# Attention's first loads, norm and projections moved into the last recurrent steps of a four-block kernel

## The chip, the cores and the metric

One core of a Trainium2 chip runs the whole program. The time is device microseconds (us) of that core, the median of several runs. Beside it stands one execution that the hardware profiler recorded.

## The reference

Three recurrent blocks (RWKV-like, width 512, 32 heads of 16) are followed by one cross attention over a context of 1024 rows; batch 4, 512 tokens, all float32. Cut to what matters here:

```python
x = block0(x); x = block1(x); x = block2(x)      # norm, token shift, lora mixes, r k v g w, scan, group norm, Wo, norm, FFN
a = layer_norm(audio_kv, ln_gamma, ln_beta)       # (4, 1024, 512): depends on the context alone, not on x
Q = (x @ Wq.T), K = (a @ Wk.T), V = (a @ Wv.T)    # 16 heads of 32
scores = einsum('bhtd,bhsd->bhts', Q, K) * scale, masked with -inf
out = softmax(scores) @ V @ Wo.T
return x + tanh(gate) * out
```

The norm of the context, K and V can be computed before the recurrent blocks are done; Q of batch 0 needs the first batch's x alone.

## The kernel before, in words

Everything is laid out by hand: each engine's instructions stand in program order, and semaphores tie them together. No scheduler decides anything.

**Recurrent part.** 24 units (3 layers, 2 time halves, 4 batches; `ITS` is 24) go through a software pipeline: in step `s` (from -1 to 25) unit `s+1` is normed, mixed and projected (`norm_a`, `lora`, `stream`), unit `s` is scanned (`products`, `updates`, `outputs`, `normed_back`), unit `s-1` has its output product and second norm (`out_product`, `norm_c`), and unit `s-2` its FFN (`feed`). In step 23 the first of these is empty, in step 24 the first two, and in step 25 only the FFN of the last unit is left. The weights (1 MB each) come through three slots on GpSimd's queue; activations are loaded and stored on SyncE's queue (SP), the finished units to a DRAM tensor `xs`.

**Attention.** Its buffers (`AT_AT`, `k_side`, `q_side`) lie over those of the recurrent part. `FIRST` lists batch 0's preparing tiles: two means, the variance, two spreads of 1/std (`rstd0`, `rstd1`), the first K tiles `k00`, `k01`, the first Q tile `q0`, and eight V tiles `v0` to `v7`; a tile is one PSUM bank that TensorE fills. K and Q come in four column groups per batch (`k{e}0`, `k{e}1`, `q{e}`); each group serves four heads, and 4 token blocks times 4 heads make 16 **turns** of a group, 64 of a batch, 256 in all (`HEADS`). A turn is `scores` (2 matmuls), maximum on VectorE, exponential on ScalarE, and three turns later eight transposes (`turned`); each fourth turn has `weighted`. Before a group's first turn its K and Q, split by ScalarE and VectorE into two rounded parts (`first_part`, `second_part`), are copied head by head into `k_side` and `q_side` by 16 + 16 small DMAs (`side_by_side`), all on SP's queue. Everything else for the later groups and the next batch is slipped in between turns: the table `BESIDE` says after which turn which tile is filled, and which engine work follows. Keys are (block, head); (10, 2) is turn 42 of the batch.

SP's queue in the attention of batch b is: side copies of groups 1, (store of the batch before), 2, 3, then the next batch's context (2 MB, `load_context`), x for its queries, mask, x for the residual, and the side copies of the next batch's group 0.

**Start.** GpSimd builds `ident` and `blk` and zeroes three large buffers; its last memset counts to `const_ready`, for which TensorE, VectorE, ScalarE and SP wait before anything else.

Of the kernel before, what the change touches and what calls it, by code (L numbers as in the profile page):

```python
# [13 lines left out]
P = 128  # L14
# [54 lines left out]
BESIDE = {(0, 2): [(0, "k10")], (1, 0): [(0, "k11")], (1, 2): [(-1, "wo0")], (2, 0): [(-1, "wo1")], (2, 2): [(0, "q1")], (3, 0): [(-1, "wo2")],  # L69
# [4 lines left out]
FIRST = ["mean0", "mean1", "var", "rstd0", "rstd1", "k00", "k01", "q0"] + [f"v{n}" for n in range(ST)]  # L74
PARTS = [f"{w}{e}{n}" for e in range(KT) for w, n in (("k", 0), ("k", 1), ("q", ""))]


def beside(n):
    if not 0 <= n < HEADS:
        return []  # L80
    b, u, h = n // (TT * KT * HPT), n // HPT % (TT * KT), n % HPT
    return [(b + off, name) for off, name in BESIDE.get((u, h), ()) if 0 <= b + off < B]

# [52 lines left out]
CONSTS = 11  # L136


def laid_out():
# [15 lines left out]
    for i, name in enumerate(("th", "thg", "tdh", "st_a")):  # L155
# [11 lines left out]
         "wv": (14320, SLOT), "wq": (16368, SLOT), "vals": (18416, ST * 384), "vals3": (21488, 2 * ST * P), "k_part": (23536, 2 * SK), "q_part": (25584, 2 * T),  # L167
         "astd": (26608, SQ), "mx": (26864, 8), "den": (26880, 2 * HPT), "rden": (26888, HPT), "rb": (26896, 2 * P), "rt": (27152, P), "ay": (27504, KT * T), "ao0": (29552, KT * T),
         "ao1": (31600, KT * T), "xq": (33648, KT * T), "probs": (48048, 4096)}
# [81 lines left out]
def build(nc, a):  # L251
    ctx = ExitStack()
    with ctx:
# [87 lines left out]
        const_ready = sem("const_ready")  # L341
        start_loaded = sem("start_loaded")
# [64 lines left out]
        at_loaded = sem("at_loaded")  # L407
# [6 lines left out]
        side_loaded = [sem(f"side_loaded{n}") for n in range(2)]  # L414
# [14 lines left out]
        def side_at(group):  # L429
            return 16 * 2 * HPT * HPT * (group // 2 + 1)  # L430
# [17 lines left out]
        def _(sp):  # L448
# [3 lines left out]
            sp.dma_start(part_of("s_first"), a["s_first"]).then_inc(start_loaded, 16)  # L452
            sp.dma_start(small_w, a["small"][0]).then_inc(small_loaded, 16)
# [21 lines left out]
            def load_vm(it, pair):  # L475
                if pair == 0:
                    sp.wait_ge(*b_ring.empty_at(it, "VT1"))
                    if it:
# [6 lines left out]
            sp.wait_ge(const_ready, CONSTS)  # L485
            load_x1(0)
            load_xl(1)
            for s in range(ITS + 2):
                e, c, b, n = s - 2, s - 1, s, s + 1
                if b < ITS:  # L490
                    load_vm(b, 0)
                if 1 <= n < ITS - 1:
                    load_xl(n + 1)
                if b < ITS:
                    load_vm(b, 1)
                if e >= 0:
                    store_x(e)
                if 0 < b < ITS:
                    load_x1(b)
                if n < ITS and n % UNITS_PER_LAYER == UNITS_PER_LAYER - 1 and n + 1 < ITS:  # L500
                    for name in ("w2g1", "td2_1"):
                        sp.wait_ge(a_ring.full, a_ring.full_at(n, name))
                    sp.dma_start(small_w, a["small"][layer_of(n + 1)]).then_inc(small_loaded, 16)
# [29 lines left out]
            def side_by_side(group):  # L533

                b, e = group // KT, group % KT
                sp.wait_ge(*d_ring.empty_at(b, f"k{e}1"))
# [3 lines left out]
                for g in range(HPT):  # L540
                    for h in range(HPT):
                        to, of = slice(AD * g, AD * g + AD), slice(AD * h, AD * h + AD)
                        sp.dma_start(k_side[group % 2][to, h, :], k_part[of, K_PART[g], :]).then_inc(side_loaded[group % 2], 16)
                sp.wait_ge(*d_ring.empty_at(b, f"q{e}"))
                for g in range(HPT):
                    for h in range(HPT):
                        to, of = slice(AD * g, AD * g + AD), slice(AD * h, AD * h + AD)
                        sp.dma_start(q_side[group % 2][to, h, :], q_part[of, Q_PART[g], :]).then_inc(side_loaded[group % 2], 16)  # L548
# [5 lines left out]

            sp.wait_ge(x_stored, X_STORED)
            load_context(0)
            for n, name in enumerate(("wk", "wq", "wv", "wo")):
                sp.dma_start(view(name), a["at_w"][n]).then_inc(at_loaded, 16)
            sp.dma_start(lnp[:], a["at_ln"]).then_inc(at_loaded, 16)
            sp.dma_start(gate[:, 0:1], a["gate"]).then_inc(at_loaded, 16)  # L560
            load_xq(0)
            load_mask(0)
            side_by_side(0)
# [17 lines left out]
        def _(pe):  # L581
# [216 lines left out]
            for n in ("s1", "m1", "s2", "i1"):  # L798
                norm_a(0, n)
            for s in range(-1, ITS + 2):  # L800
                e, c, b, n = s - 2, s - 1, s, s + 1
                has_e, has_c, has_b, has_n = 0 <= e < ITS, 0 <= c < ITS, 0 <= b < ITS, n < ITS
                if has_e:
                    feed(e, "fr", 0)
                    feed(e, "fk", 0)
                if has_b:
                    products(b, "P0a")
                    products(b, "P0b")
                if 0 < n and has_n:
                    norm_a(n, "s1")  # L810
                if has_b:
                    values_by_token(b)
                if 0 < n and has_n:
                    norm_a(n, "m1")
                if has_b:
                    products(b, "P1")
                    products(b, "P2a")
                if has_e:
                    feed(e, "fr", 1)
                if has_b:  # L820
                    products(b, "P2b")
                if 0 < n and has_n:
                    norm_a(n, "s2")
                if has_c:
                    out_product(c, 0)
                if has_b:
                    products(b, "P4a")
                if 0 < n and has_n:
                    norm_a(n, "i1")
# [1048 lines left out]
```

## Time and profile before

| | us |
|---|---|
| median of 3 runs | 3555.29 (3549.32 to 3556.19) |
| profiled execution, its own time | 3555.04 |
| its span, first to last instruction | 3553.2 |
| TensorE busy | 3326.4 (94%) |
| VectorE busy | 2632.3 (74%) |
| ScalarE busy | 1861.2 (52%) |
| GpSimd busy | 109.9 (3%) |
| mean granted clock of TensorE | 0.968 |

The span is what the change is counted in: the run's own time is 1.84 us longer than it. Busy shares are means over stages with different limits, so the rows further down are read by stage. The recurrent part ends at 2504.95 with TensorE's last FFN matmul, the first score matmul starts at 2595.12, and attention goes on to the end.

### The profile page before, as it was taken

To read this page: it belongs to the slowest core of one execution; us is meant where nothing else is said; L and a number is where in the kernel's file an instruction comes from. 1 tells how busy PE (TensorE), PEld (TensorE's weight loads), DVE (VectorE), ACT (ScalarE), POOL (GpSimd) and SP (SyncE) were. 2 spreads that over 40 slices of the span, in tenths; PEclk is the share of its full clock that TensorE was granted. 3 is DMA by queue.
4 is the path that set the end of the run, shared out by engine and by line. 5 is a ranking of instruction groups with operands and counts; after the bars stand their busy time and mean duration, and the time that the engine had idled before them with its cause. 6 is when DMAs were issued, how large, how long until landed. Compare 5 with 4: busy or idle time off the path is not lost.

```text
span 3553.2 us, 74824 instructions
## 1 busy us (share of the span) xinstructions
PE 3326.4 (94%) x31856; PEld 2507.2 (71%) x31856; DVE 2632.3 (74%) x3721; ACT 1861.2 (52%) x3087; POOL 109.9 (3%) x204
## 2 busy tenths in 40 slices
PE   6899999999999999999999999996697997997998
PEld 4667777778787777777878777775355565665666
DVE  3788888888888888888888888875155565465566
ACT  2455554555555555555555555443155555555555
POOL 1000000000000000000000000000000000000000
PEclk9899999999999999999999999998799999999999
DMA  3113332232333333233233223222324133132221
GB/s 119 60 67 108 108 120 96 105 134 91 107 117 108 108 108 109 102 123 120 90 108 116 97 108 120 94 97 78 110 54 107 48 75 94 37 84 85 60 70 51
DMA packets 91914, 336.65 MB, mean 95 GB/s; under 512 B 16704, under 2 KB 37824, under 8 KB 65600
## 3 DMA queue, kind: packets, MB, share of 16 engines
q0 software_dynamic: 27648, 201.34, 15.7%
q1 hardware_dynamic: 63936, 130.52, 12.6%
q8 instruction: 255, 4.18, 0.5%
q14 instruction: 75, 0.61, 0.1%
HBM read 252.11 MB, written 16.78 MB: 76 GB/s over the span
## 4 chain that ended last, share of the span: by engine, by line
PE 86%; DVE 6%; ACT 3%; SPq 2%; DMA 2%; issue 1%; POOL 0%; ACTq 0%; DVEq 0%; POOLq 0%
PE psum L704 39%; PE psum L713 5%; PE psum L773 5%; PE psum L750 4%; PE psum L976 4%; PE psum L952 3%; PE psum L942 3%; PE psum L994 3%; PE psum L966 2%; SPq L548 2%; PE psum L957 2%; PE psum L948 2%; PE psum L659 2%; DVE psum L1734 1%; PE psum L669 1%; PE psum L609 1%
## 5 line engine op out<-in xcount | busy, mean ns | idle before, releaser
L704 PE MATMUL psum<-rw 128*128 128x256 f32 x6144 | 1421.7, 388 | 19.5 <-DVE rw L1435 10.6
L704 PEld LDWEIGHTS psum<-rw 128*128 128x128 f32 x6144 | 1172.8, 194 | 234.5 <-issue 52.8
L1547 DVE TENSOR_TENSOR rw<-rw 128x2048 f32<-128x2048 f32 x192 | 429.5, 2279 | 18.7 <-ACT rw L1151 16.7
L1734 DVE CUSTOM_DVE_ANT_0 psum<-psum,mem 128x1024 f32<-128x1024 f32 x256 | 313.5, 1225 | 114.1 <-PE psum L966 114.0
L1310 ACT ACTIVATE rest<-psum,mem 128x1024 f32<-128x1024 f32 x256 | 284.9, 1113 | 72.7 <-DVE mem L1734 70.8
L976 PE MATMUL psum<-ident,rest 128*128 128x128 f32 x2048 | 272.7, 276 | 3.9 <-DVE mem L1704 3.8
L976 PEld LDWEIGHTS psum<-ident,rest 128*128 128x128 f32 x2048 | 236.7, 142 | 44.2 <-issue 13.5
L1096 ACT ACTIVATE rw<-psum 128x512 f32<-128x512 f32 x192 | 111.5, 593 | 297.3 <-PE psum L704 297.1
L1429 DVE SCALAR_TENSOR_TENSOR rw<-psum,rw 128x256 f32<-128x256 f32 x480 | 196.4, 477 | 72.6 <-PE psum L659 52.8
L1034 ACT ACTIVATE rw<-rw 128x256 f32<-128x256 f32 x192 | 99.8, 590 | 273.5 <-DVE rw L1379 273.5
L966 PE MATMUL psum<-side 128*128 128x512 f32 x512 | 212.3, 496 | 30.5 <-ACT rest L1310 22.6
L1303 ACT ACTIVATE mem<-psum 128x512 f32<-128x512 f32 x256 | 151.8, 593 | 159.3 <-PE psum L976 159.3
L713 PE MATMUL psum<-rw 128*128 128x512 f32 x432 | 220.7, 612 | 14.4 <-DVE rw L1517 8.4
L1530 DVE TENSOR_TENSOR_SCAN rw<-rw 128x2112 f32<-128x2112 f32 x48 | 218.7, 4556 | 16.5 <-ACT rw L1134 16.5
L1134 ACT ACTIVATE rw<-psum 128x512 f32<-128x512 f32 x192 | 197.7, 1141 | 28.5 <-PE psum L750 28.4
L773 PE MATMUL psum<-rw 128*32 128x128 f32 x6144 | 200.2, 277 | 6.1 <-DVE rw L1547 6.1
L1739 DVE COPY mem<-psum 128x512 f32<-128x512 f32 x256 | 176.0, 687 | 35.6 <-PE psum L976 35.4
L1151 ACT ACTIVATE rw<-rw 128x1024 f32<-128x1024 f32 x96 | 191.6, 2070 | 0.0
L773 PEld LDWEIGHTS psum<-rw 128*32 128x32 f32 x6144 | 161.4, 111 | 37.8 <-issue 17.4
L750 PE MATMUL psum<-rw 32*32 32x128 f32 x6144 | 180.8, 274 | 1.2 <-ACT rw L1134 1.2
L1812 POOL DMA_DIRECT2D rw<-big_dram x192 | 101.5, 529 | 2355.0 <-PE psum L704 2342.5
L750 PEld LDWEIGHTS psum<-rw 32*32 32x32 f32 x6144 | 142.0, 105 | 41.4 <-issue 39.1
(149 smaller groups left out, 4389.7 us busy)
## 6 DMA issues: line engine op xcount, KB each, us to landing
rw<-big_dram POOLq DMA_DIRECT2D x192, 1024.0 KB, 5.1
side<-mem SPq DMA_DIRECT2D x256, 128.0 KB, 2.4
rw<-xs_dram SPq DMA_DIRECT2D x32, 512.0 KB, 3.3
side<-mem SPq DMA_DIRECT2D x256, 64.0 KB, 2.0
rw<-rw SPq DMA_DIRECT2D x192, 64.0 KB, 1.9
xs_dram<-rw SPq DMA_DIRECT2D x24, 512.0 KB, 2.7
rw<-x_dram SPq DMA_DIRECT2D x16, 512.0 KB, 3.3
mem<-ctx_dram SPq DMA_DIRECT2D x4, 2048.0 KB, 8.1
```

Of the source, the lines that this page charges most:

```text
L704: last = mm(t[:, o * TC:(o + 1) * TC], big[:, k, P * m:P * m + P], src[:, k, 0:TC], start=k == 0, stop=k == KT - 1, skip_group_check=True)
L713: b_ring.fill(mm(t, blk, src, start=True, stop=True), it, name)
L750: last = mm(t[32 * g:32 * g + 32, k, :, :, s], k_t[rows, s, 256 * pair + at:256 * pair + at + 32], v_m[rows, s, :, at:at + 32], start=True ...
L773: last = mm(t[32 * q:32 * q + 32, o, s, :], rz[:, k, c, 32 * m:32 * m + 32], s_bd[:, half, NM * i + m, :], start=False, stop=c == 3, skip_ ...
L966: last = mm(t[:, sh, :], q_side[group % 2][:, h, P * q:P * q + P].bitcast(F32R), k_side[group % 2][:, h, sh * 512:sh * 512 + 512].bitcast( ...
L976: last = nc.tensor.transpose(tokens(t, o), tokens(probs[:, n % HPT, :], first + o), ident[:])
L1134: b_ring.empty(f(to, t, ACT.Copy), it, f"U{pair}{q}")
L1310: s_ring.empty(f(probs[:, n % HPT, :].rearrange("p (a s) -> p a s", a=2), s_ring.bank(n, "s"), ACT.Exp, scale=-1.0, bias=mx[:, n % 8:n % 8 ...
L1429: last = stt(to[:, m, :], t[:, o * TC:(o + 1) * TC], par(layer, MAAS, KT * FAN[s] + m), sxa[:, m, :], ALU.add, ALU.mult)
L1530: state_dve.inc(nc.vector.tensor_tensor_scan(s_flat, d_flat, s_flat, 0.0, ALU.mult, ALU.add), it, f"scan{pair}")
L1547: state_dve.inc(tt(s_bd[:, half, :, :].rearrange("p c (h j) -> p c h j", h=4), own, place, ALU.mult), it, f"b{k}{half}")
L1734: maxima.inc(nc.vector.tensor_tensor_reduce(t, t, mbias.rearrange("p (a s) -> p a s", a=2), 1.0, 3.4e38, ALU.add, ALU.min, accum_out=mx[:, ...
```

## The change

1. **Start.** The three memsets of `v_m`, `rz`, `d_in` move behind the first three weight loads on GpSimd's queue and get a semaphore of their own (`zeroed`), which only their first users await. ScalarE now waits at its start for five small loads instead of three (the norm parameters `lnp` and `gate` are loaded there), and computes tanh(gate) there.
2. **First loads.** Context, `wk` and mask of batch 0 are issued on ScalarE's queue at the start of step 23; `wv`, `wq` and the query x on SP's queue before step 24's store; `wo` after the recurrent loop. Buffers are rearranged so that these lie over what is free by then.
3. **First tiles.** Batch 0's means are filled in step 23 before the second half of `fv`, the variance, `q0` and `rstd` at its end; `k00`, `k01` and `v0` to `v4` in step 24. `v5` to `v7` of each batch move into the next 64 turns, after turns 0, 1 and 2.
4. **Side copies.** The 256 K copies go to GpSimd's queue, behind all weight loads; the 256 Q copies stay on SP's. Their semaphores are split (`k_laid`, `q_laid`).
5. **The table and SP's order.** `BESIDE` is keyed by turn and spreads the tiles differently; the next batch's context load is issued ahead of the side copies of group 3.

```diff
-BESIDE = {(0, 2): [(0, "k10")], (1, 0): [(0, "k11")], (1, 2): [(-1, "wo0")], (2, 0): [(-1, "wo1")], (2, 2): [(0, "q1")], (3, 0): [(-1, "wo2")],
...
+BESIDE = {0: [(0, "v5")], 1: [(0, "v6")], 2: [(0, "v7")], 4: [(0, "k10")], 6: [(0, "k11")], 8: [(0, "q1")], 10: [(-1, "wo0")], 14: [(-1, "wo1")],
...
+FIRST = ["mean0", "mean1", "var", "q0", "rstd0", "rstd1", "k00", "k01"] + [f"v{n}" for n in range(5)]
...
# SP: new, called in step 24 ahead of store_x; then side_by_side(0)
+            def next_loads():
+                last = ITS - 1
+                sp.wait_ge(b_ring.full, b_ring.full_at(last, "P4d"))
...
+                sp.dma_start(view("wv"), a["at_w"][2]).then_inc(at_loaded["wv"], 16)
+                sp.wait_ge(b_ring.full, b_ring.full_at(last, "KT1"))
+                sp.dma_start(view("wq"), a["at_w"][1]).then_inc(at_loaded["wq"], 16)
+                sp.wait_ge(o_ring.full, o_ring.full_at(last, "O1"))
+                sp.wait_ge(x_stored, 16 * (ITS - UNITS_PER_LAYER + B + 1))
+                load_xq(0)
# SP: attention
             for b in range(B):
                 side_by_side(KT * b + 1)
+                side_by_side(KT * b + 2)
                 if b:
                     store(b - 1)
-                side_by_side(KT * b + 2)
+                if b + 1 < B:
+                    load_context(b + 1)
                 side_by_side(KT * b + 3)
                 if b + 1 < B:
-                    load_context(b + 1)
                     load_xq(b + 1)
                     load_mask(b + 1)
# TensorE
-            pe.wait_ge(at_loaded, 6 * 16)
-            for name in FIRST:
-                batch_tile(0, name)
+                if s == ITS - 1:
+                    batch_tile(0, "mean0")
+                    batch_tile(0, "mean1")
                 if has_e:
                     feed(e, "fv", 1)
...
+                if s == ITS - 1:
+                    batch_tile(0, "q0")
+                    batch_tile(0, "rstd0")
+                    batch_tile(0, "rstd1")
# ScalarE
+            def first_loads():
+                last = ITS - 1
+                act.wait_ge(a_dve.sem, a_dve.at(last, "mix_g"))
...
+                nc.scalar.dma_start(view("an"), a["ctx"][0]).then_inc(cx_loaded, 16)
+                nc.scalar.dma_start(view("wk"), a["at_w"][0]).then_inc(at_loaded["wk"], 16)
+                nc.scalar.dma_start(mask_u, a["mask"][0:1, :].broadcast_to((P, SK))).then_inc(mask_loaded, 16)
...
+                if s == ITS - 1:
+                    first_loads()
                 if has_e:
                     feed(e, "fr", 0)
# VectorE, step 23: ahead of scan(b, 1), and at the step's end
+                if s == ITS - 1:
+                    centred(0, 0)
+                    centred(0, 1)
...
+                if s == ITS - 1:
+                    inverse(0)
                 if has_c:
                     norm_c(c, "mix")
                 if has_b:
                     gated(b, 0)
                     gated(b, 1)
+                if s == ITS - 1:
+                    after(0, "q0")
+                    scaled(0, 0)
+                    scaled(0, 1)
# GpSimd
-            nc.gpsimd.memset(part_of("v_m"), 0.0)
-            nc.gpsimd.memset(part_of("rz"), 0.0)
-            nc.gpsimd.memset(part_of("d_in"), 0.0).then_inc(const_ready, 1)
             for turn, (it, which) in enumerate(weights):
+                if turn == NSLOT:
+                    nc.gpsimd.memset(part_of("v_m"), 0.0).then_inc(zeroed, 1)
+                    nc.gpsimd.memset(part_of("rz"), 0.0).then_inc(zeroed, 1)
+                    nc.gpsimd.memset(part_of("d_in"), 0.0).then_inc(zeroed, 1)
...
+            for group in range(GROUPS):
+                b, e = group // KT, group % KT
+                if group >= 2:
+                    pool.wait_ge(s_ring.full, s_ring.full_at(HPT * TT * (group - 1) - 1, "s"))
+                elif group == 1:
+                    pool.wait_ge(x_stored, X_STORED)
+                pool.wait_ge(*d_ring.empty_at(b, f"k{e}1"))
+                for g in range(HPT):
+                    for h in range(HPT):
+                        to, of = slice(AD * g, AD * g + AD), slice(AD * h, AD * h + AD)
+                        nc.gpsimd.dma_start(k_side[group % 2][to, h, :], k_part[of, K_PART[g], :]).then_inc(k_laid[group % 2], 16)
```

On TensorE, from step 24 to the first scores, before. `L704` is a projection of the recurrent part, `L598`, `L620`, `L604`, `L609` the second norm; `L931` the means, `L922` the variance, `L936` rstd, `L942` K, `L948` Q, `L952` V, `L966` scores:

```order
L704 MATMUL psum<-rw 128x256 x56
L598 MATMUL psum<-rw,ones 32x256 x4
L704 MATMUL psum<-rw 128x256 x8
L620 MATMUL psum<-rw 128x256
L604 MATMUL psum<-rw,ones 32x64 x16
L609 MATMUL psum<-rw,pick 128x64 x4
L704 MATMUL psum<-rw 128x256 x48
L931 MATMUL psum<-mem,ones 128x512 x8
L922 MATMUL psum<-mem,ones 32x256 x16
L936 MATMUL psum<-mem,pick 128x256 x4
L942 MATMUL psum<-mem 128x512 x8
L952 MATMUL psum<-mem 128x512 x32
```

The same stretch of TensorE now, where `L718` is the recurrent projection, `L612`, `L634`, `L618`, `L623` the second norm, `L848` K, `L858` V and `L878` scores:

```order
L718 MATMUL psum<-rw 128x256 x24
L848 MATMUL psum<-mem 128x512 x8
L718 MATMUL psum<-rw 128x256 x32
L612 MATMUL psum<-rw,ones 32x256 x4
L858 MATMUL psum<-mem 128x512 x4
L718 MATMUL psum<-rw 128x256 x8
L634 MATMUL psum<-rw 128x256
L858 MATMUL psum<-mem 128x512 x4
L618 MATMUL psum<-rw,ones 32x64 x16
L858 MATMUL psum<-mem 128x512 x4
L623 MATMUL psum<-rw,pick 128x64 x4
L858 MATMUL psum<-mem 128x512 x8
```

Two K tiles and five V tiles now stand between step 24's matmuls, and 48 of `L718` (step 25) follow directly, with the scores behind them.

On SP's queue, in the attention of batch 0, before (`L543` K copies, `L548` Q copies, `L509` context, `L518` x, `L514` mask):

```order
L543 DMA side<-mem 32x1024 x16
L548 DMA side<-mem 32x512 x16
L543 DMA side<-mem 32x1024 x16
L548 DMA side<-mem 32x512 x16
L543 DMA side<-mem 32x1024 x16
L548 DMA side<-mem 32x512 x16
L509 DMA mem<-ctx_dram 128x4096
L518 DMA mem<-xs_dram 128x4x256 x2
L514 DMA mem<-mask_dram 128x1024
```

And now (`L527` Q copies, `L493` context, `L502` x, `L498` mask):

```order
L527 DMA side<-mem 32x512 x32
L493 DMA mem<-ctx_dram 128x4096
L527 DMA side<-mem 32x512 x16
L502 DMA mem<-xs_dram 128x4x256 x2
L498 DMA mem<-mask_dram 128x1024
L502 DMA mem<-xs_dram 128x4x256 x2
```

The context load now stands ahead of the last 16 Q copies, and no K copies stand on this queue.

## Rows read from the trace of the kernel before

**Rows 1.** start:end length, busy PE PEld DVE ACT POOL, granted clock, DMA share, GB/s

```profile
2504.95:2527.86 22.91, 0.01 (x1) 0.00 (x0) 1.38 (x2) 0.02 (x1) 0.00 (x0) 0.58 0.84 326
2527.86:2595.12 67.26, 56.65 (x145) 25.56 (x145) 14.18 (x10) 17.92 (x30) 0.00 (x0) 0.81 0.23 55
2349.09:2435.07 85.98, 65.91 (x743) 49.77 (x741) 65.46 (x78) 41.87 (x60) 2.22 (x5) 0.87 0.24 81
2435.07:2479.90 44.83, 33.18 (x179) 28.06 (x179) 12.82 (x21) 12.32 (x21) 2.11 (x4) 0.84 0.32 106
```

**Rows 2.** Timeline between the parts: start, duration, engine and line, idle before and releaser

```profile
2527.86 9.52 PE L931 MATMUL psum<-mem,ones 128*128 128x512 f32 x16 [22.91 <-DMA gate<-gate_dram]
2534.06 2.29 DVE L1695 TENSOR_TENSOR mem<-mem,psum 128x2048 f32<-128x2048 f32 x1 [27.65 <-PE psum L931]
2541.80 3.64 PE L922 MATMUL psum<-mem,ones 128*32 128x256 f32 x32 [4.41 <-ACT mem L1276]
2547.90 3.75 PE L936 MATMUL psum<-mem,pick 128*128 128x256 f32 x8 [2.46 <-DVE mem L1699]
2552.30 5.75 ACT L1285 ACTIVATE mem<-mem,lnp 128x512 f32<-128x512 f32 x8 [6.34 <-DVE mem L1704]
2555.38 9.40 PE L942 MATMUL psum<-mem 128*128 128x512 f32 x16 [3.73 <-ACT mem L1285]
2568.05 27.63 PE L952 MATMUL psum<-mem 128*128 128x512 f32 x64
2595.12 1.49 PE L966 MATMUL psum<-side 128*128 128x512 f32 x4
```

**Rows 3.** Timeline of step 23: second half of fv, and the start of step 24

```profile
2391.84 5.84 PE L704 MATMUL psum<-rw 128*128 128x256 f32 x16
2435.07 25.44 PE L704 MATMUL psum<-rw 128*128 128x256 f32 x112 [0.47 <-DVE rw L1384]
```

**Rows 4.** Timeline of step 24 and the start of step 25: TensorE's three gaps

```profile
2468.98 1.08 PE L604 MATMUL psum<-rw,ones 128*32 128x64 f32 x32 [3.48 <-ACT rw L1028]
2471.19 1.97 PE L609 MATMUL psum<-rw,pick 128*128 128x64 f32 x8 [1.14 <-DVE rw L1376]
2479.90 16.54 PE L704 MATMUL psum<-rw 128*128 128x256 f32 x64 [6.73 <-DVE rw L1384]
```

**Rows 5.** TensorE's waits in attention, 2595 to 3553: total us, times, longest

```profile
PE psum L931 <- DMA mem<-ctx_dram: 36.4, 3, 12.4
PE psum L922 <- ACT mem L1303: 7.4, 3, 2.5
PE psum L966 <- DMA side<-mem: 6.2, 5, 1.8
```

**Rows 6.** Timeline around turn 42 of batch 0: context load and means

```profile
2714.80 8.48 SPq L548 DMA_DIRECT2D side<-mem  x12
2723.33 0.58 SPq L509 DMA_DIRECT2D mem<-ctx_dram  x1
2731.62 10.02 PE L931 MATMUL psum<-mem,ones 128*128 128x512 f32 x16 [12.41 <-DMA mem<-ctx_dram]
```

**Rows 7.** Timeline of VectorE: first mask instruction of batches 2 and 3

```profile
3090.48 0.68 DVE L1724 TENSOR_SCALAR mem<-mem 128x1024 f32<-128x1024 uint8 x1
3343.62 0.69 DVE L1724 TENSOR_SCALAR mem<-mem 128x1024 f32<-128x1024 uint8 x1
```

**Rows 8.** DMA issues of two lines: count, min/median/max ns of issuing one

```profile
L1812 POOL DMA_DIRECT2D rw<-big_dram x192: 527/527/667, 9.4 to 2465.4; - x192
L514 SPq DMA_DIRECT2D mem<-mask_dram x4: 844/1624/5224, 2519.0 to 3233.7; - x4
```

**Rows 9.** Timeline of the start: last memset, first matmul, first activation

```profile
7.62 1.86 POOL L1803 MEMSET rw<- 128x2112 f32 x1
10.32 1.08 PE L598 MATMUL psum<-rw,ones 128*32 128x256 f32 x8 [10.32 <-DVE rw L1363]
12.83 0.38 ACT L1025 ACTIVATE rw<-psum 128x256 f32<-128x256 f32 x1
```

More of the change, by code:

```diff
@@ new lines, in _ @@
+            sp.wait_ge(const_ready, CONSTS)
+            load_x1(0)
+            load_xl(1)
+            for s in range(ITS + 2):
+                e, c, b, n = s - 2, s - 1, s, s + 1
+                if b < ITS:
+                    load_vm(b, 0)
+                if 1 <= n < ITS - 1:
+                    load_xl(n + 1)
+                if b < ITS:
+                    load_vm(b, 1)
+                if b == ITS:
+                    next_loads()
+                if e >= 0:
+                    store_x(e)
+                if 0 < b < ITS:
+                    load_x1(b)
+                if b == ITS:
+                    side_by_side(0)
+                if n < ITS and n % UNITS_PER_LAYER == UNITS_PER_LAYER - 1 and n + 1 < ITS:
+                    for name in ("w2g1", "td2_1"):
+                        sp.wait_ge(a_ring.full, a_ring.full_at(n, name))
+                    sp.dma_start(small_w, a["small"][layer_of(n + 1)]).then_inc(small_loaded, 16)
@@ L564, in _ @@
+            last_it, last = [weights[turn] for turn in range(len(weights)) if turn % NSLOT == 2][-1]
+            tiles, name = last_tile[last]
+            sp.wait_ge(tiles.full, tiles.full_at(last_it, name))
+            sp.dma_start(view("wo"), a["at_w"][3]).then_inc(at_loaded["wo"], 16)
+            sp.wait_ge(x_stored, X_STORED)
             for b in range(B):
                 side_by_side(KT * b + 1)
+                side_by_side(KT * b + 2)
                 if b:
                     store(b - 1)
-                side_by_side(KT * b + 2)
+                if b + 1 < B:
+                    load_context(b + 1)
@@ L1179, in feed, with square @@
                     f_act.inc(f(part_of("sxc")[:, cols], part_of("sxc")[:, cols], ACT.Square), it, f"kk{n}")
+            def square(b, sh):
+                act.wait_ge(*d_ring.empty_at(b, f"mean{sh}"))
+                if b and sh == 0:
+                    act.wait_ge(out_stored, 16 * KT * (b - 1))
+                    if b >= 2:
+                        act.wait_ge(d_ring.full, d_ring.full_at(b - 2, f"wo{KT - 1}"))
+                ln_act.inc(f(squares(b, sh), an[:, :, 512 * sh:512 * sh + 512], ACT.Square), b, f"sq{sh}")
@@ new lines, in deviation, with affine @@
+            def deviation(b):
+                t_ring.empty(f(astd, filled(t_ring, b, "var")[:, 0:SQ], ACT.Sqrt, bias=eps[:]), b, "var")
+            def affine(b, sh):
+                cols = slice(512 * sh, 512 * sh + 512)
+                act.wait_ge(*d_ring.empty_at(b, f"rstd{sh}"))
+                for k in range(KT):
+                    last = f(an[:, k, cols], an[:, k, cols], ACT.Identity, scale=lnp[:, k:k + 1], bias=lnp[:, KT + k:KT + k + 1])
+                ln_act.inc(last, b, f"an{sh}")
@@ new lines, in inverse_sums, with after @@
+            def inverse_sums(block_):
+                t = filled(t_ring, block_, "rb")
+                if block_:
+                    act.wait_ge(*d_ring.empty_at(block_ - 1, "out"))
+                t_ring.empty(f(rt, t[:, 0:P], ACT.Copy), block_, "rb")
+            def after(b, name):
+                if name[0] in "kq":
+                    first_part(b, name)
+                elif name == "var":
+                    deviation(b)
+                elif name[0] == "v":
+                    values_of(b, int(name[1]))
@@ L1197, in _ @@
                     feed(e, "fr", 1)
+                if s == ITS:
+                    after(0, "k00")
+                    after(0, "k01")
                 if 0 < n and has_n:
@@ L1212, in _ @@
                     norm_c(c, "s1")
+                if s == ITS:
+                    after(0, "v0")
                 if has_b:
@@ L1281, in affine @@
-            def affine(b, sh):
-                cols = slice(512 * sh, 512 * sh + 512)
-                act.wait_ge(*d_ring.empty_at(b, f"rstd{sh}"))
-                for k in range(KT):
-                    last = f(an[:, k, cols], an[:, k, cols], ACT.Identity, scale=lnp[:, k:k + 1], bias=lnp[:, KT + k:KT + k + 1])
-                ln_act.inc(last, b, f"an{sh}")
-            def first_part(b, name):
-                group = KT * b + int(name[1])
-                if group:
-                    act.wait_ge(side_loaded[(group - 1) % 2], side_at(group - 1))
-                t = filled(d_ring, b, name)
-                parts.inc(f(part(name, 0).bitcast(F32R), t, ACT.Copy, scale=-SCALE if name[0] == "q" else 1.0), b, name)
```

628 lines of the change are left out of this document (316 added, 312 removed), and 7 rows, old and new, of the table BESIDE.

## The prediction

> **What bounds the kernel now.** I read the page first: TensorE is busy 94% of the span, and no other engine is near, so time is won where TensorE stands still or runs at a low clock. Then I looked for those places by stretches and in the list of TensorE's waits. There are four.
>
> The start: nothing but GpSimd works until its last memset ends at 9.48, and the first matmul stands at 10.32 [rows 9].
>
> The passage from the recurrent part to attention: the last FFN matmul ends at 2504.95. For 22.91 us TensorE does nothing, until the DMA queue has brought the gate behind 6 MB of context and weights; then come 67.26 us of preparing tiles with 56.65 busy at a mean clock of 0.81 [rows 1, 2]. So 90.2 us pass to the first scores at 2595.12.
>
> The drain in front of it: step 23 has 86 us with 65.9 busy; it follows VectorE's chain of scans, state blocks and second norm. Step 24 has 44.8 with 33.2 busy, and its three gaps of 3.48, 1.14 and 6.73 wait for the norm of the last unit [rows 1, 4].
>
> In attention: three waits for the next batch's context, 36.4 us together [rows 5]. In batch 0 SP issues the context only when its last Q copy is out, at 2723.33, and the means wait 12.41 us for it, then run 10.02 us for 16 matmuls [rows 6]. Full-speed matmuls of that size take 27.63/64 = 0.43 each [rows 2], so 16 take 6.9: each wait costs 3.1 more through the clock.
>
> **Start: -3 us.** The three memsets are off the gate. The last, of 2112 columns, took 1.86 [rows 9], so the three with 8256 columns take an estimated 7.3; the first x, issued at the start too, must still land, so I bound the gain by 6. But ScalarE, which evacuates the first tile at 12.83 [rows 9], now waits for five loads, the last behind four others and beside 3 MB of weights that start at once. Its tanh only moves a table load. I take half, -3, between 0 and -6. What follows is a chain of dependences up to the first projections, so the shift carries on.
>
> **Passage and drain: -43.** At full speed the moved tiles cost TensorE: two means 6.9, variance 3.6, rstd 2 (half of the 3.75 seen, which is at a low clock), `k00`, `k01` 6.9, `q0` 3.4, eight V tiles 27.6, together 50.4. If they merely stood end to end, the passage would shrink by 90.2 - 50.4 = 40. I followed them through the steps instead.
>
> Step 23's front. ScalarE issues three DMAs before it empties `fr0` and the V transposes, for which TensorE waits. The trace has no DMA on ScalarE. On SP the mask's issue took 0.84 to 5.22 [rows 8], the context's 0.58 [rows 6]. Bounds 0 (slack holds it) to 6; I take 3.
>
> Step 23's middle. The means stand before the second `fv`, which took 5.84 for what costs 3.6 warm [rows 3]; the low clock falls on the means, so `fv` ends 7 later. VectorE does `unit_out` of it before its state blocks: they come 6 later. Then `centred` twice, 4.6 (2.29 each [rows 2]), stands ahead of the second scan, which was ready: +10.8. ScalarE's squares of the context, ahead of the second norm, add 1.6.
>
> Step 23's end. `q0` waits for xq, which is issued only when the last O tile is full, so it may come 2 or 3 us after `normed_back`; then `rstd1` needs the bank of `q0`, which VectorE empties only after inverse (under the 2.46 that `L936` waited for it [rows 2]), mixes and gating. Counting `q0` 3.4, its two splits 1.3, the spread 1 to 2 and the wait for xq, the first `fr` of step 24 comes about 9 later behind `normed_back` than it did at 2435.07 [rows 3]. ScalarE's affine passes of 5.75 [rows 2] come before it empties that `fr`: +1.6.
>
> Step 24. `k00`, `k01` and `v0` are pure addition, 6.9 + 3.4. `v1` fits into the gap of 3.48, `v2` overfills that of 1.14 by 1.5, `v3` and `v4` (6.9) fill that of 6.73 [rows 4]. Step 25 and the mask's bias are unchanged.
>
> Sum: 3 + 12.4 + 9 + 1.6 + 10.3 + 1.7 = 38, so the recurrent part ends near 2543, and the scores start 0.9 behind, when VectorE has emptied the last tile. Q and K copies were issued in step 24; they are hidden. The first scores come 90.2 - 38.9 = 51.3 earlier. `v5` to `v7` then cost 3 x 3.45 = 10.3 between turns, of which 2 fall into ramp-up waits: -43. Bounds: -30 (the chain of step 23 grows by 12 more) to -54.
>
> **Attention: -46 and -7.** The next context is now issued at turn 34, once `k31` is filled, with no copies ahead. From batch to batch 253.1 us pass [rows 7]; without the context's 15.3, 24 tiles of 3.45 and 12.5 for means, variance and rstd, 64 bare turns take 142.5, or 2.2 each. Eight turns and `q3` are 21 us. The context landed 8.3 after its issue (2723.33 to 2731.62, [rows 6]), so even at twice that it is there for the means at turn 42. That gives back 36.4 [rows 5] + 3 x 3.1 = 46, between 36 and 50. The variance moves one turn further from the means, so the 7.4 in which TensorE waited there go [rows 5], and of the 6.2 for side copies perhaps some; I take -7 for both, between 0 and -12.
>
> The K copies cost nothing if GpSimd is not slow. Its issue takes 0.527 [rows 8], SP's 8.48/12 = 0.71 [rows 6], so 16 take 8 to 11 us. Between `k11` (turn 6) and turn 16 are 10 turns and `q1`, 25 us. ScalarE waits for a group's landed K before it splits the next group's, 12 turns later. `q1` at turn 8 has 8 turns, 18 us, for 1.3 of splitting, 11.3 of issues and the landing. That is the tightest place, and only in batch 0, since the others have two output tiles there.
>
> The Trainium skill (DMA: Bandwidth & Descriptors, sections on the anatomy of one DMA and on SWDGE vs HWDGE) speaks against moving the copies: on GpSimd's path the descriptors are written by software, with about 2.0 us fixed per DMA plus the bytes at 436 GB/s, and VectorE can lock GpSimd out of that memory. If that were paid one after another, 2.3 each would be an estimate of 37 us per group, and the sum would come to about 3482. By the row the 192 weight issues stayed at 0.527 to 0.667 while VectorE was 74% busy, so I keep the sum; for 16 small ones in a row no trace here shows it.
>
> **Sum.** 3555.0 - 3 - 43 - 46 - 7 = 3456. The run's own time lies 0.3 below the median of 3555.29, so this is the median's forecast as well.
>
> **Rivals.**
> *The drain pays more.* Tiles set into chains are delayed by two PSUM banks and by in-order ScalarE and VectorE; 12 to 25 more gives 3468 to 3481. For it: step 23 is 66 of 86 busy but its gaps are short waits of a chain. Against: step 24 is plain matmuls.
> *Everything fits.* The low clocks of the drain (0.87, 0.84 [rows 1]) are cured by the filling, and step 23's inserted VectorE work finds slack: 15 less, 3441.
> *K copies come late on GpSimd.* A K copy costs p there, one after another. The four windows of a batch (turns 6 to 16, 18 to 32, 34 to 48, 54 to 64, with their tiles) are 32, 41, 45 and 39 us. At p = 2.3 only group 1 is late, by 5 to 11: 3482.
> *The kernel becomes slower by them.* 99 us over some 3.75 batches are 26 per batch; 64p - 157 = 26 gives p = 2.9 us. From there on the change loses. That is over five times the row's 0.527 [rows 8].
> *The context isn't earlier.* If it is still waited for (store or Q copies ahead hold SP), 46 stay: 3502.
>
> **Numbers.** Forecast (3446 to 3466) 0.50; drain pays more 0.22; everything fits 0.14; K copies late 0.06; context not earlier 0.04; slower 0.02; about the same 0.02 (gains cancelled). The range 3436 to 3484 takes in the first four and what the bounds above leave open on the low side; 0.08 and the far tails stay outside. Faster by over 0.2% (7 us, about what a measurement of this kernel can tell from no change) 0.96, within it 0.02, slower 0.02.
>
> **What would show it.** First matmul near 5, first activation near 10. End of the last FFN matmul at 2540 (2543 less the start's gain), first scores within 1 to 2 us behind. No wait of TensorE for the context over 1 us; batch to batch about 236. POOL's side copies near 0.5 to 0.7 each. Wrong it would be if scores of a group wait for the side copies, if `q0` or `rstd1` holds TensorE for over 8 us, or if ScalarE's three DMAs delay step 23 by over 6.

## The result, and the profile after

| | before | after |
|---|---|---|
| median, us | 3552.31 (3547.9 to 3556.19, 4 runs) | 3444.63 (3439.03 to 3445.73, 4 runs) |
| profiled execution, its own time | 3555.04 | 3439.03 |
| its span | 3553.2 | 3437.2 |
| TensorE busy | 3326.4 (94%) | 3294.5 (96%) |
| GpSimd busy | 109.9 (3%) | 234.2 (7%) |
| granted clock | 0.968 | 0.983 |

The ratio is 0.9694, with a 95% interval of 0.9677 to 0.9712: 107.7 us less. The forecast was 3456, with 3436 to 3484 as its range. The profiled execution is the fastest of its four; another one, of kernel 1 below, has a span of 3443.5. The profiled spans differ by 116.0, and I split that by two marks: VectorE's mixing in step 23 (2351.42 before, 2350.60 after) and the first scores.

| | before | after | difference | forecast |
|---|---|---|---|---|
| start of the span to the mark in step 23 | 2351.4 | 2350.6 | -0.8 | -3 |
| from there to the first scores | 243.7 | 181.5 | -62.2 | -51.3 |
| attention | 958.1 | 905.1 | -53.0 | -44.7 |

(-44.7 is the prediction's -46 - 7, and its +10.3 - 2 for `v5` to `v7`.) In kernel 1's profile the three differences are +3.9, -62.1 and -51.5: the last two repeat, the first does not.

The busy times by stretch: steps 23, 24 and 25, then attention (columns as in [rows 1]).

```profile
2348.26:2451.84 103.58, 83.92 (x807) 59.02 (x806) 75.87 (x88) 47.30 (x65) 2.24 (x5) 0.84 0.37 129
2451.84:2508.66 56.82, 54.83 (x235) 36.46 (x234) 14.85 (x19) 19.82 (x36) 9.86 (x20) 1.00 0.42 121
2508.66:2532.12 23.46, 21.24 (x98) 18.09 (x97) 3.70 (x8) 6.87 (x10) 0.00 (x0) 1.00 0.20 44
2532.12:3437.20 905.08, 847.66 (x7592) 575.48 (x7592) 576.87 (x1045) 531.69 (x970) 115.98 (x240) 0.99 0.31 75
```

Against [rows 1], step 23 is 17.6 longer and step 24 is 12.0 longer, but step 24 now has 2 us without TensorE instead of 11.7, and a granted clock of 1.00 instead of 0.84.

The start (timeline of all engines; here and below the fences show chosen rows of a view, in its own order):

```profile
3.05 8.26 DVE L1443 COPY rw<-rw 128x128 f32<-128x128 f32 x1
4.16 1.82 POOL L1896 MEMSET rw<- 128x2048 f32 x1
5.90 3.53 POOL L1897 MEMSET rw<- 128x4096 f32 x1
9.35 1.88 POOL L1898 MEMSET rw<- 128x2112 f32 x1
11.37 1.08 PE L612 MATMUL psum<-rw,ones 128*32 128x256 f32 x8 [11.37 <-DVE rw L1443]
15.29 1.28 ACT L1062 ACT_TABLE_LOAD   x1 [15.29 <-DMA gate<-gate_dram]
16.69 0.37 ACT L1071 ACTIVATE rw<-psum 128x256 f32<-128x256 f32 x1
```

First matmul and first activation are later than before (10.32 and 12.83, [rows 9]), not earlier. The memsets no longer hold the gate, but a small copy on VectorE, the last of the start's constants (`rw<-rw` 128x128), ends only when the last memset does. Then ScalarE waits until 15.29 for the gate's load. At the first mixing of unit 0 VectorE stands at 85.32 (82.04 before).

In the kernel before, the same copy also stood in the middle of GpSimd's three weight loads, but behind the memsets, and was short:

```profile
9.43 1.71 POOL L1812 DMA_DIRECT2D rw<-big_dram  x3
10.04 0.23 DVE L1363 COPY rw<-rw 128x128 f32<-128x128 f32 x1
```

Step 23, same view. The 16 matmuls at 2400.13 are the second half of `fv`, which stood at 2391.84 [rows 3]; the last row is step 24's start, then 2435.07 [rows 3]; the scan at 2419.45 stood at 2409.93:

```profile
2350.76 1.28 ACT L1142 ACT_TABLE_LOAD   x1 [0.80 <-DVE rw L1655]
2350.99 0.38 ACTq L1299 DMA_DIRECT2D mem<-ctx_dram  x1
2351.40 0.74 ACTq L1300 DMA_DIRECT2D mem<-at_w_dram  x1
2352.17 0.94 ACTq L1301 DMA_DIRECT2D mem<-mask_dram  x1
...
2391.02 9.27 PE L837 MATMUL psum<-mem,ones 128*128 128x512 f32 x16
2400.13 3.62 PE L718 MATMUL psum<-rw 128*128 128x256 f32 x16
2403.78 0.69 DVE L1669 TENSOR_TENSOR rw<-rw,psum 128x512 f32<-128x512 f32 x1 [6.96 <-PE psum L718]
...
2415.05 4.48 DVE L1676 TENSOR_TENSOR mem<-mem,psum 128x2048 f32<-128x2048 f32 x2
2419.45 4.55 DVE L1610 TENSOR_TENSOR_SCAN rw<-rw 128x2112 f32<-128x2112 f32 x1
...
2437.97 1.25 SPq L502 DMA_DIRECT2D mem<-xs_dram  x2
2443.26 2.10 PE L798 MATMUL psum<-ident,rw 128*128 128x128 f32 x8 [3.62 <-DVE rw L1649]
2451.84 7.07 PE L718 MATMUL psum<-rw 128*128 128x256 f32 x32
```

The means stand ahead of `fv`, at a low clock (9.27 for work that takes 7.03 elsewhere; granted 0.76 from 2391.02 to 2400.13). VectorE waits 6.96 for `fv`. Then `centred` twice, 4.48, stands right in front of the second scan, which starts as soon as it is done.

Steps 24, 25 and the first scores, same view:

```profile
2460.85 2.40 PE L718 MATMUL psum<-rw 128*128 128x256 f32 x10 [1.94 <-ACT rw L1225]
2501.74 7.08 PE L858 MATMUL psum<-mem 128*128 128x512 f32 x16
2508.66 14.06 PE L718 MATMUL psum<-rw 128*128 128x256 f32 x64
2524.07 7.17 PE L718 MATMUL psum<-rw 128*128 128x256 f32 x32 [1.35 <-ACT rw L1229]
2532.12 0.70 PE L878 MATMUL psum<-side 128*128 128x512 f32 x2 [0.87 <-DVE rw L1669]
```

The gap of 6.73 in [rows 4] holds `v3` and `v4` now (7.08). The same 64 matmuls behind it take 14.06 where they took 16.54 (granted clock 1.00 and 0.85). And of the 90.2 us between last FFN and first scores 0.87 is left.

Attention: TensorE's waits over its whole length (total, times, longest), and around batch 1's means SP's queue and TensorE:

```profile
PE psum L878 <- ACT rest L1275: 20.7, 36, 3.6
PE psum L848 <- DVE mem L1722: 6.5, 12, 0.5
PE psum L848 <- DVE mem L1693: 6.2, 3, 2.1
PE psum L842 <- DVE mem L1722: 4.5, 6, 1.0
PE psum L848 <- ACT mem L1247: 3.9, 3, 1.3
```

```profile
2640.60 0.33 SPq L493 DMA_DIRECT2D mem<-ctx_dram  x1
2653.80 10.67 SPq L527 DMA_DIRECT2D side<-mem  x16
2660.43 7.03 PE L837 MATMUL psum<-mem,ones 128*128 128x512 f32 x16
```

All three waits of [rows 5] are gone: context 36.4, variance 7.4, side copies 6.2. New ones stand in their place: the K tiles (`L848`) and rstd (`L842`) wait 21.2 in all, where they waited 5.3. The context is issued 19.8 ahead of its first reader (8.3 in [rows 6]), and the means run at full speed. From batch to batch 233.6 and 233.9 us pass, where it was 253.1 [rows 7].

The copies, in the page's costliest groups and its list of DMA issues:

```profile
L1919 POOL DMA_DIRECT2D side<-mem x256 | 123.7, 492 | 736.9 <-DVE mem L1693 619.3
side<-mem POOLq DMA_DIRECT2D x256, 128.0 KB, 4.3
```

GpSimd issues a K copy in 0.49 us and waits for its data the rest of the time.

### The profile page after: what moved, and what is told of

It is laid out like the page before. It is cut to its first block, busy times and chain, and to the rows that moved or that the text cites. A ratio compares the mean times of both kernels' runs of the same rounds, so it can differ in the third digit from the quotient of the medians.

```text
span 3437.2 us, 74851 instructions
## 1 busy us (share of the span) xinstructions
PE 3294.5 (96%) x31856; PEld 2491.6 (72%) x31856; DVE 2639.9 (77%) x3721; ACT 1860.6 (54%) x3086; POOL 234.2 (7%) x460
## 4 chain that ended last, share of the span: by engine, by line
PE 90%; DVE 6%; ACT 3%; issue 1%; DMA 0%; SPq 0%; ACTq 0%; DVEq 0%
PE psum L718 40%; PE psum L727 5%; PE psum L787 5%; PE psum L888 5%; PE psum L764 5%; PE psum L906 3%; PE psum L858 3%; PE psum L848 3%; PE psum L878 3%; DVE psum L1717 2%; PE psum L863 2%; PE psum L673 2%; PE psum L683 1%; PE psum L623 1%; PE psum L661 1%; PE psum L659 1%
## 5 line engine op out<-in xcount | busy, mean ns | idle before, releaser
L718 PE MATMUL psum<-rw 128*128 128x256 f32 x6144 | 1412.6, 386 | 14.6 <-DVE rw L1515 11.3
L718 PEld LDWEIGHTS psum<-rw 128*128 128x128 f32 x6144 | 1166.5, 193 | 227.2 <-issue 55.4
L878 PE MATMUL psum<-side 128*128 128x512 f32 x512 | 211.7, 494 | 23.0 <-ACT rest L1275 20.7
L1919 POOL DMA_DIRECT2D side<-mem x256 | 123.7, 492 | 736.9 <-DVE mem L1693 619.3
```

Source lines behind the costliest of these rows:

```text
L718: last = mm(t[:, o * TC:(o + 1) * TC], big[:, k, P * m:P * m + P], src[:, k, 0:TC], start=k == 0, stop=k == KT - 1, skip_group_check=True)
L878: last = mm(t[:, sh, :], q_side[group % 2][:, h, P * q:P * q + P].bitcast(F32R), k_side[group % 2][:, h, sh * 512:sh * 512 + 512].bitcast( ...
```

## The experiments

Each kernel was timed in five rounds beside the kernel before on the same chip. Kernels 1 to 4 shared one chip (before: 3553.54), 5 to 8 another (3555.55), 9 to 11 a third (3556.74); between chips the ratios are the fair comparison. All of them compute the whole result. Edits are against the kernel after, but for the fifth.

**1. The kernel after once more.** No edit.

> The changed kernel once more, as the mark for the runs beside it on this chip: 3440 to 3446.

3443.78 (3441.15 to 3445.7), ratio 0.9692 (0.9677 to 0.9708). Step 23's mark lies at 2355.33, 4.7 later than in the first profile; from it to the first scores 181.6 pass (181.5), and attention takes 906.6 (905.1). So stretches behind the mark repeat within 1.5 us, and the long recurrent part varies by more.

**2. The old start.** Memsets first and in the common gate, three loads, tanh behind the recurrent loop:

```diff
+            nc.gpsimd.memset(part_of("v_m"), 0.0)
+            nc.gpsimd.memset(part_of("rz"), 0.0)
+            nc.gpsimd.memset(part_of("d_in"), 0.0).then_inc(const_ready, 1)
             for turn, (it, which) in enumerate(weights):
-                if turn == NSLOT:
-                    nc.gpsimd.memset(part_of("v_m"), 0.0).then_inc(zeroed, 1)
...
-            act.wait_ge(start_loaded, 16 * 5)
-            f(gate[:, 1:2], gate[:, 0:1], ACT.Tanh).then_inc(gate_ready, 1)
+            act.wait_ge(start_loaded, 16 * 3)
```

> The changed kernel with the start as before: memsets ahead of the weight loads and in front of the common gate, ScalarE waits for three loads, tanh(gate) after the recurrent loop. Theory (the moved memsets hold up VectorE's last constant, and later places of low clock pay the 4 us back): first matmul at 10.3 and first activation at 12.8 again, 3.9 earlier than in the changed kernel, and yet the total within 5 us of the changed kernel's. Rival (the new start is worth its 3 us): 3 us or more slower than the changed kernel.

3442.13 (3440.76 to 3447.86), ratio 0.9691 (0.9675 to 0.9708): no difference. First matmul and activation are at 10.33 and 12.85 again. Unit 0's first mixing stands at 82.06, 3.8 ahead of kernel 1's, and the total doesn't show it. The change's new start gains nothing.

**3. The start mended.** GpSimd waits for VectorE's constants before its loads and memsets, and nothing at the start waits for `at_ln` and the gate:

```diff
+            pool.wait_ge(const_ready, CONSTS)
             for turn, (it, which) in enumerate(weights):
...
-            act.wait_ge(start_loaded, 16 * 5)
-            f(gate[:, 1:2], gate[:, 0:1], ACT.Tanh).then_inc(gate_ready, 1)
+            act.wait_ge(start_loaded, 16 * 3)
...
+            act.wait_ge(late_loaded, 32)
+            f(gate[:, 1:2], gate[:, 0:1], ACT.Tanh).then_inc(gate_ready, 1)
             for n in range(HEADS + LAG + 1):
```

> The changed kernel, but GpSimd waits for VectorE's constants before its weight loads and memsets, and norm parameters and gate are loaded last, on a semaphore that nobody awaits until they are needed. Theory (a memset on GpSimd keeps VectorE's copy from running): the last constant takes 0.2 instead of 8.3 us, first matmul near 5, first activation near 7; if the whole chain shifts with it, 8 us faster than the changed kernel, 3437. Rival (the copy was held by the weight loads' issues, not by the memsets, or the clock takes it back): first matmul early but total within 3 us of the changed kernel.

3432.12 (3429.94 to 3441.63), ratio 0.9665 (0.9647 to 0.9684), 11.7 below kernel 1 and 10.0 below kernel 2 on the same chip; its interval still overlaps that of kernel 1 by a little, and that of kernel 10 below does not. Its timeline:

```profile
3.05 0.23 DVE L1447 COPY rw<-rw 128x128 f32<-128x128 f32 x1
4.25 1.08 PE L613 MATMUL psum<-rw,ones 128*32 128x256 f32 x8 [4.25 <-DMA rw<-x_dram]
6.27 1.28 ACT L1071 ACT_TABLE_LOAD   x1 [6.27 <-DMA rw<-s_first_dram]
7.05 3.53 POOL L1902 MEMSET rw<- 128x4096 f32 x1
9.33 1.22 DVE L1457 TENSOR_TENSOR rw<-rw,psum 128x1024 f32<-128x1024 f32 x1 [6.05 <-PE psum L635]
```

The copy takes 0.23 instead of 8.26. VectorE's next instruction, which reads one operand from PSUM, runs in its usual 1.22 in the middle of a memset.

**9 to 11. The two halves of that mending, and the mended start with kernel 4's edit.** Kernel 10 has the added wait on GpSimd alone, kernel 11 the later loads and tanh alone, kernel 9 both and the earlier `centred`.

> After, with one edit: GpSimd waits for VectorE's constants before it issues weights and zeroes buffers; the common gate still holds the loads of `at_ln` and the gate. If the 8.26 us copy on VectorE is held up by GpSimd's memsets, it is near 0.2 here, and the first matmul comes with the data of the tokens near 4.3; the first activation still waits for the gate's load till about 15. Then, if the late copy costs what the mended start won, about 3432 to 3436; if the gate's load costs it, 3443.

> After, with the other edit of the mended start alone: the loads of `at_ln` and the gate come last and nothing of the start waits for them; GpSimd's memsets run as in after. If the memsets hold up the copy, it is again near 8.3 us, first matmul near 11.4, first activation near 12.9 as in before; then about 3440 to 3443 (theory of the copy) or 3432 to 3436 (theory of the gate's load).

> The mended start and the earlier `centred` in one kernel. If their gains add (the start 11.7 us by its run, the filling 3.2 us by its trace), it takes 3443.8 - 11.7 - 3.2 = 3429, a ratio near 0.966. If the gain of the filling is lost again behind it, 3432. In the trace: first matmul near 4.3, from the vectors' end in step 23 to the first score near 178.

| | copy on VectorE | first matmul | unit 0's mixing | ratio | median |
|---|---|---|---|---|---|
| after (kernel 1) | 8.26 | 11.37 | 85.83 | 0.9692 | 3443.78 |
| 11, gate late | 8.25 | 11.35 | 82.54 | 0.9672 (0.9658 to 0.9685) | 3437.89 |
| 10, GpSimd waits | 0.23 | 4.30 | 77.53 | 0.9656 (0.964 to 0.9671) | 3435.73 |
| 3, both | 0.23 | 4.25 | 76.29 | 0.9665 | 3432.12 |
| 9, both, `centred` early | 0.23 | 4.32 | 76.45 | 0.9648 (0.9635 to 0.9661) | 3431.39 |

The copy is long exactly where the memsets run beside it. The weight loads alone don't hold it: in the kernel before they ran beside it, and it took 0.23. At unit 0's first mixing the added wait gives 8.3, the later gate 3.3, both 9.5. My expectation of the gate's load in kernel 10 was wrong: with the copy free it had landed by 6.16, so its lateness in the kernel after (14.96) went away with the same edit. Why it landed so late there the traces don't settle. The total of kernel 11 can't be told from kernel 1's, for the intervals overlap; it fell between the two ranges that I had expected. Kernel 9 has the lowest median; by the ratios (0.9648 and 0.9692) it lies 0.45% below the kernel after. From kernel 3 it can't be told, so whether the two gains add in the total (3429) or not (3432) stays open.

**4. `centred` earlier.** In step 23 VectorE centres the context before it waits for `fv`:

```diff
+                if s == ITS - 1:
+                    centred(0, 0)
+                    centred(0, 1)
                 if has_e:
                     unit_out(e, 1)
...
-                if s == ITS - 1:
-                    centred(0, 0)
-                    centred(0, 1)
```

> The changed kernel with VectorE's two centring passes of step 23 put in front of the residual of fv's second half, where VectorE waits 6.96 us, instead of in front of the second scan. Theory (VectorE's chain sets step 23, and the passes stand in it): the second scan starts 4.5 earlier, step 24 too, total 4 to 5 us less, 3440. Rival (q0's input or ScalarE's squares set the end of step 23): under 1.5 us.

3441.39 (3437.57 to 3446.22), ratio 0.9688 (0.9672 to 0.9704): the total can't tell it from kernel 1. The trace can: from mark to first scores 178.3 pass instead of 181.6, and 178.3 again in kernel 9.

```profile
2416.03 4.56 DVE L1610 TENSOR_TENSOR_SCAN rw<-rw 128x2112 f32<-128x2112 f32 x1 [0.50 <-ACT rw L1184]
```

The second scan comes 3.8 earlier behind the mark, not 4.5, as it now waits 0.50 for ScalarE. Most of the 4.48 that `centred` took was a real delay.

**5. The context alone.** The kernel before, with one line moved:

```diff
             for b in range(B):
...
+                if b + 1 < B:
+                    load_context(b + 1)
                 side_by_side(KT * b + 3)
                 if b + 1 < B:
-                    load_context(b + 1)
                     load_xq(b + 1)
```

> The kernel before, with one edit: on SP's queue the next batch's context is issued ahead of the side copies of group 3. Theory (the three context waits cost 36.4 us and some 9 of low clock, and nothing else stands behind them): the waits vanish, 3552 - 46 = 3506, or 3499 if the waits for the variance and the side copies go too. Rival (the copies behind the 2 MB load come late and open a new wait at the next group): only half of it, near 3530.

3507.42 (3506.48 to 3508.48), ratio 0.9866 (0.9853 to 0.988): -48.1 from one line. TensorE's waits in attention:

```profile
PE psum L967 <- ACT rest L1311: 22.6, 39, 2.3
PE psum L995 <- DVE mem L1740: 9.0, 14, 0.8
PE psum L923 <- ACT mem L1304: 7.4, 3, 2.5
PE psum L967 <- DMA side<-mem: 6.4, 5, 1.9
```

The context's wait is gone, and those for the variance and for side copies stay.

**6. The context back behind the copies.** The kernel after, with `load_context` behind `side_by_side(KT * b + 3)` again; the K copies stay on GpSimd, so 16 copies stand ahead and not 32.

> The changed kernel with the context load put back behind the side copies of group 3. Theory: with only 16 Q copies left in front, TensorE waits some 10 us for it three times, plus the clock: 30 to 40 us more, 3475 to 3485. Rival (moving the K copies off SP's queue would have been enough): under 10 us more.

3491.26 (3490.43 to 3494.43), ratio 0.9822 (0.9809 to 0.9836): 46.6 above the kernel after (46.2 by the ratios, against kernel 1), and attention takes 951.0, 45.9 longer. Its wait in total, and the queue:

```profile
PE psum L836 <- DMA mem<-ctx_dram: 37.3, 3, 12.8
...
2663.45 11.06 SPq L527 DMA_DIRECT2D side<-mem  x16
2674.55 0.58 SPq L493 DMA_DIRECT2D mem<-ctx_dram  x1
2682.96 9.74 PE L836 MATMUL psum<-mem,ones 128*128 128x512 f32 x16 [12.72 <-DMA mem<-ctx_dram]
```

I expected less, with half the copies ahead. The issues are only half of the delay. In the kernel after, context and first Q copy start at 2640.60 and 2653.80: 13.2 later, because the copy waits until `q3` is filled and split. So 13 us of waiting for data and 11 of issuing lie between the two places in the queue, and the context is issued 24.5 later behind the first scores (which stand at 2541.61 here). The means cost 9.74 instead of 7.03, and 37.3 + 3 x 2.7 = 45.4 explains the 45.9.

**7. The K copies back on SP.** SP issues them again, ahead of each group's Q copies, everything else as after.

```diff
+                sp.wait_ge(*d_ring.empty_at(b, f"k{e}1"))
...
+                        sp.dma_start(k_side[group % 2][to, h, :], k_part[of, K_PART[g], :]).then_inc(k_laid[group % 2], 16)
                 sp.wait_ge(*d_ring.empty_at(b, f"q{e}"))
```

> The changed kernel with the 256 K copies back on SP's queue, each group's ahead of its Q copies, all else as in the change. Theory (the K copies were never in the way once the context goes first): within 4 us of the changed kernel. Rival (the gain beyond the forecast in attention comes from GpSimd's second queue): 8 us or more slower, with waits of scores for side copies.

3442.8 (3440.0 to 3443.03), ratio 0.9682 (0.9669 to 0.9696): no difference, and TensorE waits for no side copy. So GpSimd's queue isn't what removed those waits. The table's order is what is left of the change that could; it was not tried alone.

**8. The early loads without the filling.** Loads stay where the change put them, but TensorE's, ScalarE's and VectorE's work on batch 0's first tiles goes behind the recurrent loop, and with it SP's issues of the first side copies:

```diff
-                if s == ITS - 1:
-                    batch_tile(0, "mean0")
-                    batch_tile(0, "mean1")
...
+            for name in FIRST:
+                batch_tile(0, name)
             for n in range(HEADS + LAG + 1):
```

> The changed kernel with its early loads, but batch 0's first tiles (means to v4) put back between the recurrent part and the scores. It tells the early loads from the filling of the drain. Theory: the drain is as long as before (155.9 from step 23 to its end), the tiles start at once, and take 40 of matmuls (50.4 less three V tiles) plus 15 of waits among themselves and for the first side copies: first scores some 28 later than in the changed kernel: 3470. So of the 63 us won before the first scores, 35 are loads and V tiles moved on, and 28 are filling. Rival (filling only moves work): within 5 us of the changed kernel.

3466.09 (3459.33 to 3467.91), ratio 0.9746 (0.9732 to 0.9759): 22.3 above kernel 1 (19.2 by the ratios). From mark to first scores 206.4 pass, against 243.7 before and 181.5 after. In the timeline the means follow the last FFN matmul with no wait, but the norm's chain shows itself:

```profile
2509.89 7.03 PE L836 MATMUL psum<-mem,ones 128*128 128x512 f32 x16
2521.34 3.64 PE L820 MATMUL psum<-mem,ones 128*32 128x256 f32 x32 [4.41 <-ACT mem L1218]
2536.08 9.16 PE L847 MATMUL psum<-mem 128*128 128x512 f32 x16 [4.12 <-ACT mem L1227]
```

Of the 62.2 that the passage and drain gave, 37.3 come from early loads and from the three V tiles of batch 0 that moved on, and 24.9 from filling the drain. The V tiles' part, an estimated 10.3 (3 x 3.45), is no gain: attention pays it again.

## Why the prediction was right where it was, and where not

The order of things held: two sources of nearly all the gain, the passage and the context, with the start and the copies next to nothing. The 3456 was 11 too high. "The drain pays more" was the wrong way; "everything fits" (3441) was nearer to the result than the forecast, but only half of its mechanism held: the filling did cure low clock (0.84 to 1.00 in step 24), while the inserted VectorE work found no slack (kernel 4). That its number came close is in part luck.

**Start, -3: wrong in sign.** The step that failed is "The three memsets are off the gate". They were off the semaphore, but still held a copy that the gate waits for. At unit 0's mixing the kernel after is 3.3 behind (85.32 and 82.04); that it has made this good by step 23's mark is the fall of low clock (the 16 matmuls at 142.71 took 5.41 before, and the same ones, at 143.28, 3.72 after), for in kernel 1, the same program, the mark stands 3.9 later than before. The other half of the step, that ScalarE waits for five loads, was right: without it kernel 11 stands 3.3 earlier at unit 0's mixing, though kernel 10 shows the load in time once the copy is free. "First matmul near 5" came true in the mended start, at 4.25. Against the kernel before, which is what my term counted from, that start is 6.1 earlier at the first matmul and 5.75 at unit 0's mixing (76.29 and 82.04), so the bound of 6 was right. The 11.7 of kernel 3 counts from the late start of the kernel after, 9.5 of it at unit 0's mixing; the rest is no more than the recurrent stretch varies by.

**Step 23's front, +3: 0.** The three issues took 2.06 together and lie beside ScalarE's table load of 1.28 and its next activations. They held nothing.

**Step 23's middle, +12.4: 11.6.** The order was as forecast: low clock on the means, VectorE's wait for `fv`, `centred` in front of a scan that was ready. The second scan came 10.3 later behind the mark (forecast 10.8). Kernel 4 confirms the part of `centred`.

**Step 23's end, +9: 6.0.** `q0` did not wait for xq: SP issued that at 2437.97, and `q0` ran at 2445.16, right behind `normed_back` (2443.26 + 2.10). The "2 or 3 us" for it were the excess.

**Step 24, 1.6 + 10.3 + 1.7 = 13.6: 12.0.** The stall of 1.94 at 2460.85 is the affine passes' 1.6. `v3` and `v4` fit the gap of 6.73 nearly to the us. The step's granted clock rose from 0.84 to 1.00, which may be the 1.6 that is missing; no run parts the two.

**Step 25, 0: -2.5.** This I left out: with the gap ahead of it filled, the same 64 matmuls ran at a granted clock of 1.00 and not 0.85, in 14.06 and not 16.54. I had weighed it as a rival and not as a term.

Sum of these: 17.6 + 12.0 - 2.5 = 27.1 in place of 38, and that is the 10.9 by which the passage beat its forecast.

**Context, -46: right.** Kernel 5 gives 48.1 alone and 46.9 in attention's length: there TensorE stands still 34.4 less and is busy 12.5 less, where I had 36.4 and 9.3. Kernel 6 gives 46.6 back.

**Variance and side copies, -7, and `v5` to `v7`, +8.3: together -6.1 instead of +1.3.** That is the step in attention's length from kernel 5 (911.2) to the kernel after (905.1), and the term that was mis-sized. Both waits went wholly (7.4 and 6.2), and I had halved them without a reason in the rows. But that doesn't make up the sum term by term. TensorE's idle time fell by only 10.0 (67.4 to 57.4), because the new table brought the waits at K tiles and rstd, 15 more than in kernel 5, and took some 10 from others; and its busy time rose by only 3.9 (843.8 to 847.7), though the three V tiles alone take 9.5 more. Which move of the table did what stays open.

**K copies on GpSimd, 0: right,** and kernel 7 shows that SP could have kept them. The rule of the Trainium skill that I weighed (DMA: Bandwidth & Descriptors, anatomy of one DMA and SWDGE vs HWDGE) is borne out in its direction: a K copy lands 4.3 us after its issue on GpSimd, and 2.4 after it on SP in kernel 7. The 4.3 is more than the 2.3 that I had worked out from the page, and the measurement decides. But it is time to landing, which overlaps from copy to copy, and not 2.3 us of queue each: the queue took 0.49.

## What to carry to other kernels

Ask of each wait what stands ahead in the queue, and also what those instructions wait for. The context's load cost 46 us where it stood behind copies that waited for a tile it had nothing to do with, and one moved line gave that back. When work leaves a gate, look at what else the engines before the gate share with it: here a semaphore was freed, and a copy that the gate still needs was held by the same memsets. Count a start's gain from the kernel that you compare with, not from the one that went wrong. And when a gap is filled by useful work, look for a gain behind it too: here 2.5 us of step 25, by the clock.

## What the hardware showed unexpectedly

**A GpSimd memset stops a small VectorE copy.** 128x128 float32 from SBUF to SBUF took 8.26 us beside GpSimd's loads and three memsets and 0.23 without, and it was not let in between one memset and the next (its end, 11.31, is that of the third, 11.23, and not of the first, 5.98). The loads alone did not hold it (0.23 beside them in the kernel before). Yet its row begins at 3.05, 1.1 ahead of the first memset at 4.16, and what it waited for until then the rows don't show. An addition on VectorE with one operand in PSUM ran through unhurt (1.22). The Trainium skill says that GpSimd and VectorE lock a shared pair of ports for a whole instruction, and that a VectorE instruction takes part if it runs in a two-port mode or reads two SBUF inputs while the GpSimd instruction reads SBUF (SBUF — State Buffer, two separate sides). Kernels 3, 10 and 11 fit such a lock, with 0.23, 0.23 and 8.25. That the copy ran in a two-port mode no run here shows by itself.

**Equal code, up to 13 us apart.** Between unit 0's mixing and step 23's mark nothing differs in the kernels, yet that took 2261.9 us in kernel 11 and 2275.2 in kernel 6. TensorE's busy time for the same matmuls is 2236.5 in the one and 2249.9 in the other, at a granted clock of 0.99 and 0.98, so nearly all of the difference is low clock. Five rounds don't resolve a 3 us edit in such a total; a stretch between two marks does (181.5 to 181.8 in eight traces with that code, 178.3 in both with `centred` early).
